# A two-layer transformer on one core: another order of work between the layers

## The reference

```python
for layer in (0, 1):
    xn = layernorm(x)
    x = x + attention[layer](xn) + ffn[layer](xn)
```

## Time and profile before

| | us |
|---|---|
| runs of the kernel before | 546.1, 543.2, 544.37; median 544.37 |
| the profiled execution, whole | 545.68 |
| its span in the profile | 543.9 |
| TensorE busy, matmuls (2919) | 503.1, 92% |
| VectorE busy | 359.2, 66% |
| ScalarE busy | 314.8, 58% |
| GpSimd busy | 302.9, 56% |

### The profile page before, as it was taken

The page is one execution under the profiler, slowest core; times in us unless marked ns, Lnnn a source line. Parts: engine busy times, 40 slices in busy tenths (PEclk is TensorE's granted clock), DMA queues, the critical chain, the costliest instruction groups (busy, mean ns, idle before and its releaser), DMA issues.

```text
span 543.9 us, 9756 instructions
## 1 busy us (share of the span) xinstructions
PE 503.1 (92%) x2919; PEld 385.5 (71%) x2919; DVE 359.2 (66%) x1036; ACT 314.8 (58%) x745; POOL 302.9 (56%) x234
## 2 busy tenths in 40 slices
PE   8999799889899999999999999999988789899972
PEld 6666688779688888788888888888664335566651
DVE  6999665548666476385484581524569959998735
ACT  1265277577876675776775865756322368475520
POOL 1046468878877575675676576643033055788420
PEclk9999999999999999999999999999999889999995
DMA  7992669998798687687686696862686021544345
GB/s 218 342 337 59 168 147 210 220 233 189 177 233 221 182 175 159 128 187 163 144 190 142 147 204 134 181 130 30 171 264 233 0 74 60 114 100 109 79 103 197
DMA packets 84147, 89.12 MB, mean 164 GB/s; under 512 B 27008, under 2 KB 71360, under 8 KB 83712
## 3 DMA queue, kind: packets, MB, share of 16 engines
q1 hardware_dynamic: 64592, 59.16, 38.2%
q0 software_dynamic: 17376, 27.24, 27.0%
q10 hardware_dynamic: 2128, 2.10, 1.1%
HBM read 65.34 MB, written 21.29 MB: 159 GB/s over the span
## 4 chain that ended last, share of the span: by engine, by line
PE 54%; DVE 15%; issue 11%; DMA 8%; ACT 6%; POOL 4%; SPq 0%; DVEq 0%; POOLq 0%; ACTq 0%
PE bank L988 9%; PE bank L576 6%; PE bank L997 4%; PE bank L996 4%; PE bank L1227 4%; PE bank L568 3%; PE bank L533 3%; DMA expert_sums<-expert_weights,token_of_slot 2%; PE bank L978 2%; POOL expert_sums L958 2%; PE bank L585 2%; PE bank L1245 2%; ACT normed L656 2%; PE bank L551 2%; PE bank L521 2%
## 5 line engine op out<-in xcount | busy, mean ns | idle before, releaser
L958 POOL DMA_INDIRECT expert_sums<-expert_weights,token_of_slot x79 | 136.3, 1725 | 56.0 <-ACT expert_weights L1020 33.4
L950 POOL DMA_INDIRECT expert_weights<-normed_x,token_of_slot x79 | 85.1, 1077 | 53.6 <-DVE expert_weights L966 18.3
L988 PE MATMUL bank<-expert_weights 128*88 128x128 f32 x632 | 82.6, 273 | 2.0 <-issue 1.6
L988 PEld LDWEIGHTS bank<-expert_weights 128*88 128x88 f32 x632 | 72.8, 156 | 3.3 <-issue 3.3
L576 PE MATMUL bank<-out_weights,expert_weights 128*128 128x256 f32 x256 | 59.9, 380 | 2.2 <-DVE residual L847 1.5
L576 PEld LDWEIGHTS bank<-out_weights,expert_weights 128*128 128x128 f32 x256 | 46.5, 190 | 9.1 <-ACT expert_weights L693 3.8
L804 DVE SCALAR_TENSOR_TENSOR expert_weights<-bank,blocks_valid 128x64 f32<-128x64 f32 x32 | 7.2, 224 | 63.7 <-ACT expert_weights L670 54.2
L996 PE MATMUL bank<-expert_weights 88*128 88x256 f32 x158 | 47.1, 379 | 0.0
L997 PE MATMUL bank<-expert_weights 89*128 89x256 f32 x158 | 47.1, 379 | 0.0
L1020 ACT ACTIVATE expert_weights<-bank,chosen_bf 128x256 f32<-128x256 f32 x79 | 37.8, 479 | 14.9 <-PE bank L997 9.9
L1190 POOL DMA_INDIRECT tiles<-normed_x,token_of_slot x23 | 27.1, 1179 | 32.6 <-DVE token_of_slot L1184 20.0
(11 more groups left out here) (279 smaller groups left out, 1073.6 us busy)
## 6 DMA issues: line engine op xcount, KB each, us to landing
expert_weights<-experts_out SPq DMA_DIRECT2D x79, 192.8 KB
expert_weights<-experts_in SPq DMA_DIRECT2D x79, 176.0 KB
expert_weights<-L_ffn_wi SPq DMA_DIRECT2D x32, 128.0 KB
expert_weights<-w_comp SPq DMA_DIRECT2D x1, 2048.0 KB, 11.9
expert_weights<-fold_g SPq DMA_DIRECT2D x1, 2048.0 KB, 14.9
expert_sums<-zeros SPq DMA_DIRECT2D x2, 1024.0 KB, 20.8
expert_weights<-L_ffn_wo SPq DMA_DIRECT2D x16, 128.0 KB
normed_x<-normed SPq DMA_DIRECT2D x2, 896.0 KB, 6.1
```

Source lines behind the costliest of these rows:

```text
L950: nc.gpsimd.indirect_dma_start(xt0[g % 4], None, xn0, bass.IndirectOffsetOnAxis(ap=MAP[:, g:g + 1], axis=0)).then_inc(gathered[g % 4], 16)
L958: nc.gpsimd.indirect_dma_start(sums0[g % 2], bass.IndirectOffsetOnAxis(ap=MAP[:, g:g + 1], axis=0), yt0[g % 4], None, compute_op=ALU.add). ...
L988: ins = nc.tensor.matmul(ps[5][0:DHB, c * P:(c + 1) * P], w[:, k * DH + c * DHB:k * DH + (c + 1) * DHB], xT0[g % NXT][:, k * P:(k + 1) * P ...
```

## The change

Nothing that is computed changes. The order and some of the plumbing of layer 1's start do:

1. The sums are loaded as four DMAs, first half of both, then second half of both; VectorE norms tiles 0 to 3 before it adds the second halves.
2. TensorE turns a token tile and makes the values of the tile before; product (0,0) comes ahead of the turn of tile 7.
3. VectorE chooses experts as soon as logits are there; `rope_qk(0, 0)` comes ahead of the slots, ropes (0,1) and (0,2) and all of half 1 behind the map's read. TensorE has the map product right behind product (1,0), after 6 warming matmuls on zeros; product (1,1), `angles(0)` and product (1,2) follow.
4. `angles(1)` and its turns move from before tile 0 to behind beat 3 on TensorE; ScalarE runs beats 0 to 3 before `take_angles(1)` and the first sine. Its sines and squares of token tile t come at beats 3t+1 and 3t+2 (before: 3t-1 and 3t), its second roots behind beat 6 (before: 4).
5. On VectorE `middle(0)` stands ahead of `norms`, and `middle(1)` behind `differences(0)`; then before each `middle(g)` come the head parts that a list `PARTS1` names.
6. The bias comes into the projection's bank by a matmul with the identity; POOL's addition goes, and project1's bank 4 becomes bank 2.
7. Rows of `xn1` and `rows1` are numbered partition by partition, so loads and stores have runs of 2 KB and more in HBM instead of 1 KB.

```diff
+PARTS1 = [max(g - 1, 0) + (g >= 9) + (g >= 16) for g in range(NT1)]
...
         def project1(pe, b):
-            pe.wait_ge(oT_sb, b + 1)
-            pe.wait_ge(hT_sb, NT0 + NT1)
...
+            bank = ps[PROJB[b % 2]]
             for j in range(TPB):
+                nc.tensor.matmul(bank[:, j * HID:(j + 1) * HID], IDN[:, :], BO, start=True, stop=False)
+                if j == 0:
+                    pe.wait_ge(oT_sb, b + 1)
                 for k in range(KC):
...
             for t in range(NT - 1):
                 turn_tokens(pe, t)
-            for t in range(NT - 1):
-                values_router(pe, t)
+                if t > 0:
+                    values_router(pe, t - 1)
+            values_router(pe, NT - 2)
+            queries_keys(pe, 0, 0)
             turn_tokens(pe, NT - 1)
-            queries_keys(pe, 0, 0)
             values_router(pe, NT - 1)
             queries_keys(pe, 0, 1)
             queries_keys(pe, 0, 2)
+            rank_pe(pe, E1, ps[2], 1)
             queries_keys(pe, 1, 0)
-            rank_pe(pe, E1, ps[2], 1)
+            pe.wait_ge(op_sb, NT)
+            for i in range(N_WARM1):
+                ins = nc.tensor.matmul(ps[7][:, 0:HID], ZERO[:, 0:P], ZERO[:, 0:HID], start=True, stop=True)
+            ins.then_inc(warm, 1)
+            map1_pe(pe)
             queries_keys(pe, 1, 1)
...
             angles(pe, 0)
             queries_keys(pe, 1, 2)
             pe.wait_ge(vr_ok, 3)
             turn_angles(pe, 0)
             turn_angles(pe, 1)
-            map1_pe(pe)
-            angles(pe, 1)
             expert1_pe(pe, 0, {})
             pe.wait_ge(slots_ok, 3)
             expert1_pe(pe, 1, {})
-            turn_angles(pe, 2)
-            turn_angles(pe, 3)
...
                 expert1_pe(pe, i, e)
+                if i == 3:
+                    angles(pe, 1)
+                    turn_angles(pe, 2)
+                    turn_angles(pe, 3)
...
+        def heads_part(dve, st, t, part):
+            if part == 0 and 1 <= t < NT - 1:
+                differences(dve, t + 1)
+            meet(dve, st, t, part)
+            if (t, part) == (0, 2):
+                square_sums(dve, st, 1)
+            if (t, part) == (2, 0):
+                norms(dve, st, 1)
+            if (t, part) in ((2, 1), (3, 2)):
+                turns(dve, st, t)
...
             route_dve(dve, st, E1, K1, 1)
-            for c in range(1, NQK):
-                rope_qk(dve, 0, c)
+            take_values(dve, 1)
+            take_values(dve, 2)
+            rope_qk(dve, 0, 0)
             route_dve_slots(dve, st, E1, K1, ps[2], 1)
             map1_dve(dve, st)
             map1_experts(dve, st)
+            map1_dve_end(dve, st)
+            rope_qk(dve, 0, 1)
+            rope_qk(dve, 0, 2)
             rope_qk(dve, 1, 0)
             rope_qk(dve, 1, 1)
             square_sums(dve, st, 0)
             rope_qk(dve, 1, 2)
-            map1_dve_end(dve, st)
+            middle(dve, 0)
             norms(dve, st, 0)
             turns(dve, st, 0)
             differences(dve, 0)
+            middle(dve, 1)
             turns(dve, st, 1)
...
+            differences(dve, 1)
+            done = 0
+            for g in range(2, NT1):
+                for n in range(done, PARTS1[g]):
+                    heads_part(dve, st, n // 3, n % 3)
+                done = PARTS1[g]
+                middle(dve, g)
+            for n in range(done, 3 * NT):
+                heads_part(dve, st, n // 3, n % 3)
```

More of the change, by code:

```diff
@@ L457, in build @@
         added = [sem(f"sums_added{i}") for i in range(2)]
[L458 to L459 removed]
+        written1 = [sem(f"rows1_written{i}") for i in range(4)]
+        sum_ld = [[sem(f"sums_loaded{i}_{hf}") for hf in range(2)] for i in range(2)]
         SUMS = [YG[:, 0:NT * HID], SQ]
```

118 lines of the change are left out of this document (52 added, 66 removed).

## The result

The changed kernel takes 555.69 us (550.67 to 558.87, 4 runs) against 543.79 (542.89 to 546.1): ratio 1.0196, 95% interval 1.0155 to 1.0237. Slower, as forecast, but by 11.9 us where 3.3 were forecast, and outside the range; the interval doesn't settle whether it is 2%. The profiled execution took 556.61 (span 554.8); the kernel before's took 545.68.

What follows compares the result with a forecast made beforehand. VectorE's list was taken to bound the touched stage: sums end 2.5 us later, plus 0.8 in the tail, 3.3 on the profiled 545.68, so 549.0, or 547.7 on the median's scale; range 542.0 to 550.6.

Steps and rivals of the forecast that it cites:

- Sums, turns, index cast: Start of layer 1: last projection ends 0.75 us earlier, first query product starts 1.9 earlier, index cast takes 0.2 instead of 2.29.
- Choices ahead of ropes: VectorE's expert choices and map: slots start 5.0 us earlier, the map is ready 9.1 earlier, at 424.3.
- So of 9.1 us, 2.2 reach the tiles: TensorE behind the map: after a clock fall, tile 0's first product starts at 440.4 instead of 442.59.
- The second fall: TensorE's pause between 437.4 and 440.4, ahead of tile 0's product: clock halves again, sums end 2.4 us later; chance 0.18.
- Rival 1: A second clock fall in the pause with only two turns, product 1 and angles(1) at 1.2 GHz; 550.1 us; chance 0.18.
- VectorE's list: VectorE's tile loop: 7.54 us of norms, turns and differences uncovered behind middle(0), plus waits; sums end 2.5 later.
- The tail: From the last sum to the end: the bias's extra matmuls on TensorE lengthen the last projection, costing 0.8 us.
- the price is 0: Last projection: if the clock held, 10 instructions take 2.2 us, the rows' landing binds and the bias costs nothing.
- Layer 0, held to be the same: Everything ahead of the stage the change touches, from 380 us on: taken as unchanged, with no term in the sum.
- Rival 2: TensorE's clock doesn't fall behind the map: tiles and all behind 2.9 us earlier, 544.0 to 544.8 us; chance 0.20.
- Rival 3: TensorE, not VectorE, sets the tile loop's pace; product 2 starts before 447.5; 540.8 to 541.6 us; chance 0.18.
- Rival 4: ScalarE's table switches cost more than their row, 1.28 to 1.4 us more ahead of tile 0; 549.1 us; chance 0.02.

Runs made afterwards that it cites:

- c2: Changed kernel with norms, turns and differences of head tile 0 put back ahead of middle(0) on VectorE; 554.75 us, ratio 1.0183 to the kernel before.
- b4: Changed kernel with items 3, 4, 5 and 6 undone, so the bias is added by GpSimd again; 540.54 us, ratio 0.9932 to the kernel before.
- b3: Changed kernel with items 3, 4 and 5 undone (old map order and old tile loop); 539.91 us, ratio 0.9933 to the kernel before.
- b2: Changed kernel with only item 3 undone (old map order, new tile loop kept); 553.44 us, ratio 1.0167 to the kernel before.
- a1: The changed kernel measured again without any edit; 555.57 us, ratio 1.0200 to the kernel before.
- a2: Changed kernel with items 4 and 5 undone (old tile loop, early map kept); 548.42 us, ratio 1.0078 to the kernel before.
- b1: Changed kernel with items 4 and 5 undone, plus 9 matmuls on zeros ahead of the map's and 5 behind; 546.88 us, ratio 1.0053 to the kernel before.
- c4: Changed kernel with items 3, 4 and 5 undone, plus 6 matmuls on zeros behind the map's; 539.16 us, ratio 0.9902 to the kernel before.
- d2: Changed kernel plus 4 and 1 matmuls on zeros behind beats 0 and 1 alone; 552.56 us, ratio 1.0126 to the kernel before.
- d1: Changed kernel with matmuls on zeros around the map's alone, 9 ahead (instead of 6) and 5 behind; 552.77 us, ratio 1.0168 to the kernel before.
- c1: Changed kernel plus 13 matmuls on zeros behind the last projection, at the end of TensorE's queue; 555.06 us, ratio 1.0204 to the kernel before.
- c3: Changed kernel with angles(1), its turns and ScalarE's copy put back ahead of the first tile's product; 557.93 us, ratio 1.0254 to the kernel before.
- a4: Changed kernel with matmuls on zeros: 9 (not 6) ahead of the map's, 5 behind, 4 and 1 behind beats 0 and 1; 548.14 us, ratio 1.0080.
- a3: Changed kernel with only item 6 undone (bias by GpSimd again); 553.44 us, ratio 1.0139 to the kernel before.
- d3: Changed kernel with items 3 to 6 undone (bias by GpSimd), plus 6 matmuls on zeros behind the map's; 539.05 us, ratio 0.9916 to the kernel before.

## Why the prediction was wrong

The direction was right, and the times of the stages behind P came within 2 us each, but in part by luck: the forecast booked the early map as a gain, which the runs show to be a loss, and gave the loop's loss to a cause that c2 rules out. The sum missed 7.6 us of the profiled execution (549.0 against 556.61): 3.8 before P, where the forecast took layer 0 to be unchanged and the changed kernel's layer 0 ran later; 1.6 to the first head sum, the second fall of the clock, which the sum left out; 1.9 from there to the last sum, waits in VectorE's list that were taken too short; 0.2 in the tail. By its steps:

1. **Sums, turns, index cast: right for the stage, counted too low.** P in the kernels with the old loop is 393.8 to 396.7 (forecast 395.6), and in the changed kernel layer 0 is 3.80 late at 366 us and P only 3.03, so the gain of 0.75 is there; the first query product came 12.79 after P (forecast 12.5; before 13.61); the cast took 0.19 (before 2.29), but taking GpSimd's addition away was not needed for that: in b4 it took 0.22 with the addition there. What I did not work out is what this alone gives when the rest stays: b3 and b4 show 4 us to the last sum. In b3 `angles(0)` starts 1.7 sooner than before, the wait for the rope ahead of `angles(1)` is 2.94 and not 3.80, and less of `angles(1)` runs at half clock. What item 7 has of the 4 us no run separates.

2. **Choices ahead of ropes: the times right, the gain wrong.** The map was read 28.6 after P (forecast 28.1), the first product came at 44.72 (forecast 44.8), product (1,1) at half clock (3.78, forecast 3.4). "So of 9.1 us, 2.2 reach the tiles" is the step whose mechanism failed. With the old map order and the same loop (b2) tile 0's product comes 41.63 after P, so in a1 the early map makes it 2.8 later, not 2.2 earlier, and the last sum 2.7 later; with the old loop it costs 7.12 (a2 against b3), as TensorE's angles lose the cover of VectorE's slots and one-hots. The forecast's 44.8 was met by luck: the rest of the change gave 4.6 (46.25 before, 41.63 in b2), and that hid the loss. With the clock held it costs 7.16 (b1 against c4), so the clock is not its reason.

3. **The second fall, given 0.18.** It came. The first head sum was at 57.44 (forecast 55.8), 1.6 later; with the pause filled (d2) it was at 55.97. Rival 1 had its place and cause, the pause with two turns in it, at 2.4. With the first fall averted (d1) the second did not come either, and both together are worth 3.0 (a1 less d1; the forecast had 2.9 for the first alone, which by d2 less d1 is 2.2).

4. **VectorE's list: the waits were at their places, but mis-sized, and the loss had another reason.** Forecast 0.6, 0.6 and 1.9; measured 1.46, 1.05 and 2.33, 1.7 more in all. From the first head sum's start to the last one's end it was 72.39 (forecast 70.5). The new loop's price depends on what stands beside it: 7.7 with the old map order (b2 against b3), 3.3 beside the early map (a1 against a2), 1.5 when there the clock is held as well (d1 against b1). TensorE's stall at two parts in one gap was 2.58 at 485.33 (forecast 1 to 2), and the clock fell there a third time (the product behind it took 3.51). Neither reached the sums: from the first head sum to the last it was 72.39 with that fall and 72.54 without it (a1). My reason for the list's price, norms uncovered behind `middle(0)`, was no reason: c2 moves half of them and nothing changes. What holds the first head sum is ScalarE's squares behind `angles(1)` behind beat 3.

5. **The tail: 25.6 (forecast 25.4), but not for the bias.** In seven kernels with the bias on TensorE (a2, b1, b3, c1, c3, d1, d2) it was 24.0, as short as b4's 23.86 without it: the projection is 2.5 longer (13.8 from the last sum to VectorE's last take in b3, 11.2 in b4), but the rows' landing hides it, which the prediction had as "the price is 0" if the clock held. It held there: the windows of b3 show 1.00 for 16 us behind the last sum, where the kernel before had 0.50 from 12 us on. In the changed kernel it fell with the last sum's end (0.68 over 528 to 532, and 1.00 until 529.4), and VectorE waited 6.20 for the first take, not 4.61 as in b3. Of the ten kernels with the new loop five had no fall there (a4, c1, c3, d1, d2), and their tails are 23.98 to 24.73. So it is luck that the forecast missed by 0.2 only: the length came from a fall and not from the bias.

6. **Layer 0, held to be the same: 3.8 us in the profiled execution, the largest single miss, and its cause is open.** This is the term that the prediction put at nothing without a reason: it did not put it in question, since no instruction of layer 0 changes. TensorE in the timeline of the kernel before:

```profile
120.17 1.12 PE L533 MATMUL bank<-keys,expert_weights 128*128 128x112 f32 x8 [1.48 <-DVE expert_weights L804]
```

and of the changed one:

```profile
122.34 1.22 PE L533 MATMUL bank<-keys,expert_weights 128*128 128x112 f32 x8 [3.11 <-DVE expert_weights L804]
```

TensorE's window there, in the kernel before:

```profile
118.00:126.00 8.00, 6.52 (x45) 1.00 0.84 177
```

and in the changed one:

```profile
118.00:126.00 8.00, 4.89 (x28) 0.83 0.84 219
```

VectorE had waited for a gather that landed later (4.88 at 118.69 in the changed kernel, 2.99 at 116.51 before), TensorE waits for VectorE, and the clock falls. Nearly all of the difference arises there: the same expert product of layer 0 (L996) starts at 85.0 and 85.6, 137.7 and 141.5, 366.2 and 370.0. In 9 of the 10 profiled kernels with the new loop the clock fell near 120, and P is 398.4 in the mean of the ten; in the 8 with the old loop it never fell, and P is 395.4. The medians agree: a1 is 7.2 above a2, of which P to last sum and tail give 4.8, and b2 is 13.5 above b3, of which these give 9.3. a4_filled is the exception. Neither a longer program for TensorE (c1) nor a part of a4's filling (d1, d2) brought layer 0 back. Why the order of layer 1 should reach back to it is not shown, and as there is one profiled execution for each kernel, and the runs of one kernel differ by up to 8 us, I can't say how much of the 3 us is in every run.

**The other rivals.** Rival 2 (no fall) was wrong for this kernel, but its price of 2.9 was about right: with the clock held the kernel gains 2.8 to 3.0 (a4, d1), both falls together. Rival 3 was wrong: product 2 came 56.5 after P. Rival 4: ScalarE in the timeline of the changed kernel

```profile
440.87 1.28 ACT L1298 ACT_TABLE_LOAD   x1
442.16 0.28 ACT L1298 ACTIVATE shared_w<-expert_weights 128x96 f32<-128x96 f32 x1
```

starts the activation 0.01 us behind the load's end, as in the earlier trace rows. The drain of 1.38 us that the Trainium skill, "ScalarE: Activation LUTs" (section "What ACT_TABLE_LOAD costs"), adds to each switch is not seen here either.

**The books.** Against the kernel before, P to last sum: -4.1 (halves, turns, bias, numbering: b3), +7.1 (early map: a2 less b3), +3.3 (loop: a1 less a2), together the +6.4 of a1. In the other order the 10.4 of early map and loop divide as +7.7 (loop: b2 less b3) and +2.7 (early map: a1 less b2), so neither of the two is the one cause. With some 3 for layer 0 and up to 1 for the tail that is 10.4 of the median's 11.9.

## What to carry to other kernels

Work out each part of a change alone against the kernel before, even where the whole adds up: here a gain of 4 us hid a loss that was booked as a gain. Then take the parts away in both orders: early map and new loop cost over 7 us each alone and 10.4 together, and whoever undoes only one of them puts a wrong price on it. Before pulling a short serial step forward, ask which long step of another engine it was hiding behind or covering; the map came 8 us sooner, while TensorE's angles lost their cover. Keeping all but items 3 to 5, and filling TensorE's pause ahead of `angles(1)`, gives 539.2: 16 us faster than the change, and 1% faster than the kernel before. And before adding work to a queue, look at where in the queue it lands: behind beat 0 is ahead of tile 0's product here, and that decides what d2 shows.

## What was not expected of the hardware

- The index cast waits for GpSimd's addition to end, whatever is left of it, and then runs at once: it ended 0.05, 0.04, 0.05 and 0.04 us behind it in the kernel before, a3, b4 and d3, and took 2.29, 0.55, 0.22 and 0.22. VectorE's MAX8 instructions beside the same addition were not held (six in 0.50 to 0.51). The exclusive lock that the Trainium skill, "SBUF — State Buffer" (section "SBUF: two separate sides"), describes is held for a whole instruction while the other engine is blocked, and the trace agrees with it for the cast. To get the cast out of its way it was enough that the addition started sooner after P (b4, d3).
- The same pause of 1.76 us on TensorE, with only turns around it, was followed by half clock in the five kernels in which the clock had fallen and come back some 10 us earlier (product of 3.21 to 3.66), and by full clock in d1, where zeros had averted the first fall (1.96). Zeros in the pause itself averted the second fall too, behind the first one (d2). Whether the first fall brings the second one execution of d1 can't show.
- 12 instructions on zeros in a pause of 2.94 us kept the clock and moved the last sum by 1.30 (b3 to c4); the tail took 0.76 of it back, waiting for the experts' rows.
- Instructions that nobody changed (layer 0) took 3 us more in the mean of the kernels with the new loop, with later gathers and a fall of the clock near 120 us; why is open.
